# A recurrent attention kernel on one core: the value group of each key tile split in two halves, TensorE's program written out, five tiles of lead, and the softmax sums copied by ScalarE

## The reference

```python
xn = layernorm(x)
qkv = einsum('bld,ed->ble', xn, w_qkv)          # 16 heads of 16
q, k = rope(q), rope(k)
attn = softmax(einsum('blhd,bmhd->bhlm', q, k) * scale)
s = einsum('bhlm,bmhd->blhd', attn, v) @ w_out.T
e = argmax(xn @ gate_w.T)                       # one of 8 experts for each token
g = silu((relu(xn @ wg[e])**2 * (xn @ wu[e])) @ wd[e])
out = x + s * g
```

## Time and profile before

| | |
|---|---|
| median of 3 runs | 1640.71 (1639.81 to 1641.09) |
| profiled execution, its time | 1638.55 |
| profiled execution, its span | 1636.7 |
| granted TensorE clock, mean | 0.985 |
| PE, DVE, ACT, POOL busy | 1527.6, 1378.7, 1173.2, 150.4 |

### The profile page before, as it was taken

The page is one execution under the profiler, slowest core; times in us unless marked ns, Lnnn a source line. Parts: engine busy times, 40 slices in busy tenths (PEclk is TensorE's granted clock), DMA queues, the critical chain, the costliest instruction groups (busy, mean ns, idle before and its releaser), DMA issues.

```text
span 1636.7 us, 29614 instructions
## 1 busy us (share of the span) xinstructions
PE 1527.6 (93%) x9121; PEld 655.4 (40%) x9121; DVE 1378.7 (84%) x1530; ACT 1173.2 (72%) x2349; POOL 150.4 (9%) x198
## 2 busy tenths in 40 slices
PE   6997999979899999999999999999999999999997
PEld 4553333346333333333333333333333333333336
DVE  6778899954699999999999999999999999999706
ACT  4642677755777777777777777777777777777770
POOL 3332332000122000000010000000100000000100
PEclk9998899989999999999999999999999999999999
DMA  5873145235344343323222342222222422222303
GB/s 193 272 187 116 36 82 117 43 88 155 78 78 76 52 88 48 43 42 42 42 42 42 45 91 42 42 39 39 39 39 37 92 41 43 39 40 28 62 4 120
DMA packets 77820, 116.54 MB, mean 71 GB/s; under 512 B 29072, under 2 KB 64272, under 8 KB 70800
## 3 DMA queue, kind: packets, MB, share of 16 engines
q1 hardware_dynamic: 71808, 103.99, 32.5%
q0 software_dynamic: 3072, 8.39, 2.0%
q10 hardware_dynamic: 2896, 3.62, 0.6%
HBM read 75.31 MB, written 39.85 MB: 70 GB/s over the span
## 4 chain that ended last, share of the span: by engine, by line
PE 68%; ACT 15%; DVE 10%; issue 5%; DMA 2%; SPq 0%; DVEq 0%; ACTq 0%
PE ps L1126 27%; PE ps L1115 26%; ACT arena L578 14%; DVE arena L713 7%; PE ps L1047 3%; PE ps L1106 2%; PE ps L1048 2%; PE ps L1206 2%; PE ps L1222 1%; PE ps L1252 1%; DVE arena L679 1%; PE ps L1071 1%; DMA arena<-xs_d 1%; PE ps L1179 1%; PE ps L1058 1%
## 5 line engine op out<-in xcount | busy, mean ns | idle before, releaser
L578 ACT ACTIVATE arena<-ps 128x512 f32<-128x512 f32 x2048 | 1059.6, 602 | 302.0 <-PE ps L1115 300.8
L713 DVE TENSOR_REDUCE arena<-ps 128x1 f32<-128x1024 f32 x992 | 1167.6, 1218 | 99.9 <-PE ps L1106 94.4
L1115 PE MATMUL ps<-qs,ks 50*128 50x512 f32 x2048 | 749.6, 446 | 51.8 <-ACT arena L578 16.6
L1106 PE MATMUL ps<-ks,qs 48*128 48x512 f32 x1984 | 786.6, 471 | 11.7 <-DVE arena L713 7.8
L1115 PEld LDWEIGHTS ps<-qs,ks 50*128 50x128 f32 x2048 | 339.9, 185 | 657.1 <-issue 430.5
L1126 PE MATMUL ps<-arena 128*32 128x512 f32 x4096 | 547.9, 607 | 0.8 <-ACT arena L578 0.8
L1106 PEld LDWEIGHTS ps<-ks,qs 48*128 48x128 f32 x1984 | 327.6, 186 | 67.0 <-DVE arena L713 33.9
L1126 PEld LDWEIGHTS ps<-arena 128*32 128x32 f32 x4096 | 80.7, 108 | 132.5 <-ACT arena L578 115.2
L981 POOL COPY arena<-v_sb 128x256 f32 (+1 forms) x32 | 13.3, 417 | 1092.0 <-DVE arena L803 1076.3
L1047 PE MATMUL ps<-arena 128*128 128x512 f32 x128 | 68.1, 614 | 0.7 <-ACT arena L501 0.7
L803 DVE COPY arena<-ps 128x512 f32<-128x512 f32 x32 | 22.0, 686 | 47.6 <-PE ps L1126 47.4
(11 more groups left out here) (103 smaller groups left out, 491.9 us busy)
## 6 DMA issues: line engine op xcount, KB each, us to landing
qs<-parts_d SPq DMA_DIRECT2D x186, 128.0 KB
ks<-parts_d SPq DMA_DIRECT2D x186, 128.0 KB
parts_d<-arena SPq DMA_DIRECT2D x64, 256.0 KB, 2.6
xs_d<-arena SPq DMA_DIRECT2D x13, 384.0 KB, 3.7
arena<-xs_d SPq DMA_DIRECT2D x13, 384.0 KB, 3.8
ys_d<-arena SPq DMA_DIRECT2D x13, 384.0 KB, 2.8
onum_d<-arena SPq DMA_DIRECT2D x128, 32.0 KB
arena<-onum_d SPq DMA_DIRECT2D x3, 1024.0 KB
```

The lines of the kernel that those rows point to most:

```text
L578: nc.scalar.activation(prob[kb % 2][:, c * W:(c + 1) * W], ps[:, bank, :], ACT.Exp, scale=SCALE).then_inc(exp_done[bank], 1)
L713: nc.vector.tensor_reduce(most[head_slot][:, tile, u:u + 1], ps[:, AB + 2 * u:AB + 2 + 2 * u, :], AX.XY, ALU.max).then_inc(a_reduced[u], 1)
L1106: ins = nc.tensor.matmul(ps[:, AB + c, :], qs[head_slot][ABASE:ABASE + KR, tile * P:(tile + 1) * P].bitcast(F32R), ks[head_slot][ABASE:ABA ...
L1115: nc.tensor.matmul(ps[:, bank, :], ks[s][0:KS, kb * P:(kb + 1) * P].bitcast(F32R), qs[s][0:KS, c * W:(c + 1) * W].bitcast(F32R), start=Tru ...
```

## The change

Four things are changed. `weigh_values` is called twice in a step, each time for half of the columns of each chunk (256 of 512): its first half behind chunks 0 and 1 of the next tile's scores and their A matmuls, its second half behind chunks 2 and 3. The score of chunk 3 now belongs to the same step as its tile's other chunks (in the step before its exponentials), so the very first one is issued ahead of the pairs, and around the experts one is held back. TensorE's pairs are written out one by one, without a loop. The A stream has a lead of five tiles, not four, and the four small operations at a head's end stand one each behind four reductions. The copy of the sums moves from VectorE to ScalarE, behind the last exponential of the next head's first tile.

```diff
-    AHEAD = KB + 4
+    AHEAD = KB + 5
...
+            def sums_out(s, pi):
+
+                act.wait_ge(pv_done[1], past(pi * KB + (s + 1) * NB2))
+                act.wait_ge(spread_in[s], past(pi * 16))
+                act.wait_ge(o_stored[s], past(pi * (16 * QT)))
+                nc.scalar.copy(osb[s], ps[:, PVB, :]).then_inc(o_out[s], 1)
+
-            def exps(pi, s):
+            def exps(pi, s, first):
...
+                        if kb == 0 and c == QT - 1 and not first:
+                            sums_out(1 - s, pi - 1 + s)
...
-                if kb == 0 and not (isinstance(pi, int) and pi == 0 and s == 0):
-                    sums_out(1 - s, pi - 1 + s)
...
-                    k = 2 * (2 * (ahead - KB) + u + 1)
+                    k = 2 * (ahead - KB) + u + 1
                     if 0 <= k < CUTS and coming:
                         cut_maxima(k, pi * 2 + (s + 1), 1 - s, s, (pi + 1) * 64)
-                        cut_maxima(k + 1, pi * 2 + (s + 1), 1 - s, s, (pi + 1) * 64)
...
+            def weigh_values(pi, s, kb, half):
+
+                if kb == 0 and half == 0:
                     pe.wait_ge(v_staged[s], pi + 1)
                     pe.wait_ge(o_out[1 - s], past(pi + s))
...
+                if half == 0:
+                    for c in range(1, QT):
+                        pe.wait_ge(exp_done[b_bank(s, kb, c)], past(b_before(pi, s, kb, c) + 1))
+                lo, hi = half * W // 2, (half + 1) * W // 2
                 for c in range(QT):
...
+                    last = nc.tensor.matmul(ps[32 * c:32 * (c + 1), PVB, lo:hi], vst[s][:, kb, :],
+                                            prob[kb % 2][:, c * W + lo:c * W + hi],
+                                            start=(kb == 0 and half == 0), stop=(kb == KB - 1 and half == 1))
+                if half:
+                    last.then_inc(pv_done[kb % 2], 1)
...
+            score(0, 0, 0, QT - 1)
+
+            def pair(pi, last_pair, hold=False):
...
+                        if with_b and kb == KB - 1:
+                            pe.wait_ge(loaded[b_slot], (pi + 1 + s) * (16 * LOADS))
+                            pe.wait_ge(shift_loaded[b_slot], (pi + 1 + s) * 64)
                         for c in range(QT):
-                            if c == 0:
-                                score(pi, s, kb, QT - 1)
-                            elif with_b:
...
-                                score(b_pi, b_slot, (kb + 1) % KB, c - 1)
+                            if with_b and not (held_back and c == QT - 1):
+                                score(b_pi, b_slot, (kb + 1) % KB, c)
                             if with_a:
                                 score_a(g + AHEAD, a_slot, ahead % KB, c)
-                        weigh_values(pi, s, kb)
+                            if c % 2:
+                                weigh_values(pi, s, kb, c // 2)
...
-            with pe.Fori(0, FB) as pi:
-                pair(pi, False)
+            for pi in range(FB):
+                pair(pi, False, hold=(pi == FB - 1))
             experts()
-            with pe.Fori(FB, NP - 1) as pi:
+            score(FB, 0, 0, QT - 1)
+            for pi in range(FB, NP - 1):
                 pair(pi, False)
             pair(NP - 1, True)
```

More of the change, by code:

```diff
@@ L582, in exps @@
                             nc.scalar.copy(counts, ps[:, PVB, 0:2 * E]).then_inc(counts_out, 1)
-            for pi in range(FB):
+                        if kb == 0 and c == QT - 1 and not first:
+                            sums_out(1 - s, pi - 1 + s)
+            exps(0, 0, True)
+            exps(0, 1, False)
+            for pi in range(1, FB):
                 for s in range(2):
-                    exps(pi, s)
+                    exps(pi, s, False)
             experts()
@@ L589, in _ @@
                 for s in range(2):
-                    exps(pi, s)
+                    exps(pi, s, False)
+            sums_out(1, NP - 1)
             for n in range(0, B * ENDT, 2):
@@ L796, in invert @@
                 nc.vector.reciprocal(spread[s], spread[s]).then_inc(rec_ready[s], 1)
-            def sums_out(s, pi):
-                dve.wait_ge(pv_done[1], past(pi * KB + (s + 1) * NB2))
-                dve.wait_ge(spread_in[s], past(pi * 16))
-                dve.wait_ge(o_stored[s], past(pi * (16 * QT)))
-                nc.vector.tensor_copy(osb[s], ps[:, PVB, :]).then_inc(o_out[s], 1)
             def step(pi, last_pair, s, kb):
@@ L859, in _ @@
             pair(NP - 1, True)
-            sums_out(1, NP - 1)
             invert(1, NP)
@@ L1116, in score @@
                                  qs[s][0:KS, c * W:(c + 1) * W].bitcast(F32R), start=True, stop=True).then_inc(scored[bank], 1)
-            def weigh_values(pi, s, kb):
-                if kb == 0:
+            def weigh_values(pi, s, kb, half):
+                if kb == 0 and half == 0:
                     pe.wait_ge(v_staged[s], pi + 1)
                     pe.wait_ge(o_out[1 - s], past(pi + s))
-                for c in range(1, QT):
-                    pe.wait_ge(exp_done[b_bank(s, kb, c)], past(b_before(pi, s, kb, c) + 1))
+                if half == 0:
+                    for c in range(1, QT):
+                        pe.wait_ge(exp_done[b_bank(s, kb, c)], past(b_before(pi, s, kb, c) + 1))
+                lo, hi = half * W // 2, (half + 1) * W // 2
                 for c in range(QT):
-                    last = nc.tensor.matmul(ps[32 * c:32 * (c + 1), PVB, :], vst[s][:, kb, :],
-                                            prob[kb % 2][:, c * W:(c + 1) * W],
-                                            start=(kb == 0), stop=(kb == KB - 1))
-                last.then_inc(pv_done[kb % 2], 1)
+                    last = nc.tensor.matmul(ps[32 * c:32 * (c + 1), PVB, lo:hi], vst[s][:, kb, :],
[3 more added lines that the diff above has]
+                    last.then_inc(pv_done[kb % 2], 1)
             pe.wait_ge(pt_out, NT)
@@ L1146, in _ @@
             pe.wait_ge(counts_out, 1)
-            def pair(pi, last_pair):
+            score(0, 0, 0, QT - 1)
+            def pair(pi, last_pair, hold=False):
                 for s in range(2):
                     for kb in range(KB):
+                        held_back = hold and s == 1 and kb == KB - 1
                         g = pi * (2 * KB) + (s * KB + kb)
@@ L1158, in pair @@
                             pe.wait_ge(a_loaded[a_slot], (pi + 2) * (16 * LOADS))
+                        if with_b and kb == KB - 1:
+                            pe.wait_ge(loaded[b_slot], (pi + 1 + s) * (16 * LOADS))
+                            pe.wait_ge(shift_loaded[b_slot], (pi + 1 + s) * 64)
                         for c in range(QT):
-                            if c == 0:
-                                score(pi, s, kb, QT - 1)
-                            elif with_b:
-                                if c == 1 and kb == KB - 1:
-                                    pe.wait_ge(loaded[b_slot], (pi + 1 + s) * (16 * LOADS))
-                                    pe.wait_ge(shift_loaded[b_slot], (pi + 1 + s) * 64)
-                                score(b_pi, b_slot, (kb + 1) % KB, c - 1)
+                            if with_b and not (held_back and c == QT - 1):
+                                score(b_pi, b_slot, (kb + 1) % KB, c)
                             if with_a:
                                 score_a(g + AHEAD, a_slot, ahead % KB, c)
-                        weigh_values(pi, s, kb)
+                            if c % 2:
+                                weigh_values(pi, s, kb, c // 2)
             def turn_sorted(i):
```

## The result

The changed kernel takes 1582.83 us (median of four runs, 1576.22 to 1592.45) against 1640.86 for the kernel before beside it (1639.81 to 1641.09): ratio 0.9652 [0.9598, 0.9706], 58 us less. Once more, unchanged (experiment 12), it took 1581.65 (1578.64 to 1585.77), ratio 0.9647 [0.9631, 0.9663]. Its profiled execution is the run of 1576.22, with a span of 1574.5 and a mean granted clock of 0.976 (before: 1638.55, 1636.7, 0.985). The 62 us are the difference of these two spans. Runs over 1.5% above the fastest of their kernel (one in experiment 4, three in experiment 5) are left out of the ratios, though not out of the medians.

A forecast was written before the change was run, and what follows sets the result against it. Bound: a closed ring of 2.61 us a step, no engine full. Halving gives 2.46; gains of 63 and 9 less 2.5 for the prologue make 69.5 off 1638.55, 1569.0, with the median 2.2 above: 1571 us, range 1540 to 1610.

The forecast's parts named there:

- The ring: Steady attention before the change: closed chain of exponentials, scores and the whole value group, 2.61 us per key tile.
- the new step: Steady attention, one key tile: TensorE's own work sets the pace at 2.46 us, no wait exceeding it.
- half 0.57: Value matmuls: each group of 256 columns takes 0.57 us start to start, where the whole group takes 1.00.
- The 0.14 of a group that does not shrink: Value matmuls: fixed part of each group, 0.14 us, that halving the columns does not reduce.
- a step of 2.66 and 1673 us: Steady attention, estimate by the skill page: eight more matmuls at 25 ns add 0.2 us a step.
- Head changes: Where one head follows another: ScalarE's copy of the sums delays the first value half, 0.43 us a head, 0.86 a pair.
- The small operations at nothing: VectorE at a head's end: four small operations spread behind four reductions cost nothing; uncovered, 0.94 us a head.
- The landing of the shift: SyncE's four shift transfers after the transpose: 2.4 us left for landing, costed at nothing.
- The loop end, 0.24 a turn: TensorE's loop end: a step of 2.85 us, 0.24 over, said to disappear when the pairs are written out.
- rival 4: Straight-line TensorE code waits for instruction packets, some 105 in all; at 1.5 us each 1729 us; chance 6%.
- The clock: First four steps of pairs 0 and 1: bound by routing and slower TensorE clock, left out of the gain.
- rivals 1 and 2: VectorE becomes the bound, about 1504 us, 7%; a hand-over ends later than worked out, about 1605 us, 17%.

The follow-up runs named there:

- experiment 12: The changed kernel once more, unchanged, beside experiments 9 to 11: 1581.65 us, ratio 0.9647 to the kernel before.
- experiment 4: Changed kernel with TensorE's pairs behind the experts in a loop again, halves kept: 1747.38 us, ratio 1.0616.
- experiment 5: Changed kernel with four tiles of lead in place of five, small operations still one behind each reduction: 1643.97 us, ratio 0.9975.
- Experiments 1 and 2: Changed kernel with one whole value group, behind chunk 1 (first: 1737.91 us, ratio 1.0575) or behind all four chunks (second: 1653.85 us, ratio 1.0077).
- Experiment 6: Changed kernel with four tiles of lead and two small operations behind one reduction, as before the change: 1586.22 us, ratio 0.9699.
- experiment 3: Changed kernel with the copy of the sums back on VectorE, ahead of the head's first reduction: 1597.89 us, ratio 0.9743.
- Experiments 4 and 8: experiment 4, and the kernel before with two pairs in one pass of TensorE's loop, value groups whole: 1676.8 us, ratio 1.0214.
- experiment 10: Changed kernel with three matmuls that nothing reads added behind the experts only: 1574.8 us, ratio 0.96.
- experiment 9: Changed kernel with whole value groups in the first eight steps, halves from the ninth on: 1586.01 us, ratio 0.965.
- experiment 7: Changed kernel with nine matmuls that nothing reads, six around the prologue's A-stream tiles and three behind the experts: 1583.57 us, ratio 0.9646.

## Why the prediction was right, and by how much it missed

**The ring and the new step: right, to the digit.** Step 2.46, half 0.57, TensorE without waits within a head, pair 79.62 (forecast 79.6). Experiments 1 and 2 show that the halving is what breaks the ring: with all else in place the kernel is slower than before without it. The 0.14 of a group that does not shrink was also right. The estimate worked out from the Trainium skill ("TensorEngine Tiling (Array Packing)", Instruction Overhead), a step of 2.66 and 1673 us, did not come: the step is 2.46. It laid 0.2 for the eight more matmuls on top of a sum that already held 0.14 for them, some 18 ns each.

**Head changes: the sum right, its parts not, so partly luck.** A pair is 79.62 - 32 x 2.46 = 0.90 above its steps, where I charged 0.86. I charged 0.43 to each head for ScalarE's copy. The rows of one head change, TensorE and ScalarE:

```profile
584.77 0.50 PE L1116 MATMUL ps<-qs,ks 50*128 50x512 f32 x1
...
585.06 0.58 ACT L577 COPY arena<-ps 128x512 f32<-128x512 f32 x1
...
585.75 0.64 PE L1129 MATMUL ps<-arena 128*32 128x256 f32 x8 [0.24 <-ACT arena L577]
```

From that score to the value half are 0.98, not 0.66: 0.32 a head, since the copy starts 0.2 behind the head's last value half, not the 0.40 of the earlier trace rows. In place of the rest stands an item that I had taken for the loop's end, once per pair:

```profile
582.15 0.47 PE L1116 MATMUL ps<-qs,ks 50*128 50x512 f32 x1
...
582.54 0.18 PEld L1116 LDWEIGHTS ps<-qs,ks 50*128 50x128 f32 x1 [0.21 <-ACT arena L585]
```

The second of these two scores, here its weight load, waits until ScalarE is done with its bank; the two stand 0.39 apart, not 0.33. The two half-steps there take 1.28 and 1.39 (first scores at 580.87, 582.15 and 583.54), 0.21 more than twice 1.23. The three score banks go round by `(kb * QT + c + s) % 3`. From head 0 to head 1 that runs on; from head 1 to the next pair's head 0 it does not (bank 1 is followed by bank 0), so each of the first two scores waits for an exponential one chunk later than usual. It costs about 0.2 a pair, some 3 us in all, and 2 x 0.32 + 0.21 = 0.85 is nearly the 0.90. By this reading a rotation that runs on would remove it; that wasn't tried.

**The small operations at nothing: right.** They stand one each between reductions that follow one another by 1.21 to 1.26, not 1.14, and TensorE does not wait. Experiment 6 adds that packed in pairs they cost nothing that the time shows either. The copy moved off VectorE is worth 15 us (experiment 3); the prediction gave the move no worth of its own.

**The landing of the shift: right.** The transfers are issued from 577.07 on and the score at 582.15 does not wait for them; experiment 5 is the case that the prediction priced by "each 0.1 beyond is 0.1 a head", and there it is 1.25 a head.

**The loop end, 0.24 a turn that "disappears": misread.** The long step of the earlier trace rows belongs to the order of the banks at a change of pairs, not to the loop: it has the same length where the loop is left (1512.36 to 1515.20), its wait is for ScalarE, and there, too, it is the score of chunk 1 that comes to a bank written two chunks before. It did not disappear; it is the 0.21 above. That the pair came out right is because the copy costs 0.11 less at each of two heads, about as much. I also did not ask what a loop around the longer body would cost. Experiments 4 and 8 answer: about 5 us a turn and more than that again in clock, 165 us in all in experiment 4. The writing out is no item of 0.24; it is the condition on which the halves pay. That TensorE would wait for its program in straight-line code (rival 4) did not come: the packets rise from 22 to 107, 85 more where 105 were forecast, and outside of the low clock no step behind the experts is longer than 2.46 by more than 0.03 but those at a change of heads.

**The clock: the term that was mis-sized.** "In pairs 0 and 1 the first four steps are bound by the routing and a slower TensorE clock, and I leave them." The lower level lasts some 20 us longer than before instead, and the stretch up to the experts gives 0.5, not 6.5; the sum is in the section on the result. Behind the experts another few us go the same way (low for 13.7 from 418.3 on, before for 6.8, which is 3 at 0.43; 59.7, not 63; with the fillers of experiment 10 the same stretch is 1535.8 - 341.3 = 1194.5, that is 62.5 less than before). Both items together are 9, of which 2 come back in the projection (where the clock was low for 3.4 us before, from 1617.1 on, and is not now), and that is the gap between 1569.0 and the profiled 1576.2. The median is 6.6 above that execution, not 2.2: the four runs have clocks of 0.976, 0.977, 0.968 and 0.973, and their times roughly follow (1576.22, 1579.51, 1592.45, 1586.15).

**Two slips in the forecast's figures.** A half of 0.53 and a step of 2.38 would give 1571 - 0.08 x 508 = 1530, not the 1540 at the lower end of the range, and the chances of the forecast and of rivals 1 and 2 add up to 0.87, not 0.88.

**What stays open.** Why the clock stays at 1.2 GHz until 196.4 with TensorE busy 9 to 10 of 10 us. The halves are at most a part of it (experiment 9: with whole groups the low time is 40.9, against 47.8 and 27.3 before, and 0.5 to 1.4 of the 6.0 come back); nine more matmuls, six of them ahead of the steps, did not shorten it (experiment 7: 54.6). Open too is the length of body at which a turn begins to stall.

## What to carry to other kernels

When no engine is full and the chain is a closed ring, look for the member that stands there whole though only a part of it is needed, split it, and work out the engine's own time afterwards with every fixed cost per piece: the halves cost TensorE 0.34 a step and freed 0.49. Before making a loop's body longer, measure what one turn costs at the new length. Where a kernel's time moves by more than its sum allows, look at the granted clock by windows first; three matmuls in idle time bought 7 us here. And before a long step is put down to a loop's end, look at the same step where the loop is left.

## What was unexpected of the hardware

- A turn of TensorE's loop costs nothing that the rows show with a body of 1186 instructions, and about 5 us with 1699 (12 turns, 61.5 us) and with 2367 (5 turns, 23.7 us). The Trainium skill ("Runtime: NRT & Kernel Launch", Instruction fetch mechanics) says that a taken branch whose target isn't in the current window of two pages forces a fetch of the target's page before execution goes on. The traces agree that there is such a stall, with 141 and 85 packets in place of 22; but two of the page's blocks of 256 instructions would have put 1186 on the dear side, and its 2048 instructions for TensorE would have put 1699 on the cheap side, and the measurement decides against both.
- Straight-line code has no such stall: 107 packets, and the steady step is 2.46 throughout.
- A standstill of 1.3 us at a head (experiment 5) was followed, at 3 of 30 heads, by a stretch at 1.2 GHz (30.7, 13.7 and 6.8 us); one of 5 us at each of 12 turns (experiment 4, 10.2 to 30.7 us).
- The clock can stay at 1.2 GHz for 48 us, 148.6 to 196.4, with TensorE busy over 9 of 10 us for the last 30 of them.
